# A recurrent layer with a low-rank adapter on one core: the adapter's weight by rows of 8 KB, its bias by 8 partitions, x one block earlier

## The chip, the core and the metric

The kernel runs on one core of a Trainium2 chip. The metric is the device time of one execution, in microseconds (us). The core has a matrix engine (PE, with its weight loads shown as PEld), a vector engine (DVE), a scalar engine (ACT), a further engine (POOL) and SP, which only issues DMA transfers here. Sixteen DMA engines move the data. Each engine carries out its own instructions in order and waits on semaphores that others raise; a transfer raises its semaphore by 16 when all of it has landed.

## What is computed

The reference, cut to what matters (B = 16, T = 256, D = H = 256, rank R = 8):

```python
xz = x @ Wx + b                                   # [16, 256, 1024]
for t in range(256):                              # the recurrence
    z = xz[:, t] + h @ Wh                         # h: [16, 256], Wh: [256, 1024]
    i, f, o, g = split(z)
    c = sigmoid(f) * c + sigmoid(i) * tanh(g)
    h = sigmoid(o) * tanh(c);  hs[:, t] = h
x = x + hs
n = layernorm(cond) * gamma + beta                # [16, 256]
w = gelu(n @ W1 + bias1) @ W2 + bias2             # W2: [256, 8192], 8 MB
a1, b1, a2, b2 = split(w)                         # each [16, 256, 8], one per batch entry
u = einsum("btd,bdr->btr", x, a2)
mid = gelu(x @ base_down + einsum("btr,blr->btl", u, b2))
v = einsum("blr,btl->btr", b1, mid)
out = x + mid @ base_up.T + einsum("bkr,btr->btk", a1, v)
```

All data are float32.

## The kernel before

**The recurrence** sets the pace. Time is cut into 32 blocks of 8 steps (`one_block(k, front)` of each engine, `s` from 0 to 7; step number 8k + s). In a step PE multiplies the hidden state with `wh` (line 712) on top of a projection that ACT has copied into PSUM (`seed_bank`, `seed_o`, lines 358 and 362), DVE transposes the result (lines 868 and 872), ACT applies the tanh, DVE forms the new cell and the new hidden state (lines 878 to 893), and PE begins again. Whatever else is to be done is placed by hand behind a step's own instructions on each engine: the transposes of later x (line 483), the projection of the block after next in 8 pieces (`project`, line 502; `PIECES` says which pieces fall into which step), its evacuation on DVE (line 802), the adapter for finished blocks (lines 515 to 590), and in the first four blocks `make_weights`.

**Ahead of step 0** `wx`, `wh` and other weights are loaded, x of blocks 0 and 1 is transposed and projected (block 1: pieces 0 to 5; its last two pieces come in step 0), and the projections go through DMA from `proj` into `seed`, whose layout the recurrence needs (`load_seed`, line 255, four transfers a block).

**The adapter's weight.** In block 0 the condition is normalised (DVE and POOL, line 1011), transposed and multiplied with `w1` (line 607, step 3); ACT's gelu gives `hid` (line 387). W2 comes in quarters, in the order `QUARTERS`, into three tiles; each quarter consists of four units (column half h, row half kc). From step 11 on PE multiplies one unit a step (line 633): steps 11 to 14 take quarter 0 of that order, 15 to 18 quarter 1, 19 to 22 quarter 2, 23 to 26 quarter 3. After every second unit DVE adds the bias (line 920; first at the end of step 12, after it has waited for all of `w_bias`), and POOL issues the transfers that put the result in its place (line 1020).

**SP's queue** is one list in order, and a waiting transfer holds up all behind it. Ahead of the blocks: x, `wx`, `wh`, x, gamma, beta, seed of block 0, x of block 2, W1, its bias, up, seed of block 1, down. In block 0: W2 pieces 0 and 1, x of block 3, pieces 2 to 7 with a transfer of the bias (line 289) behind each of 2 to 5, seed of block 2. In block 1: x of block 4, pieces 8 to 12, seed of block 3. In block 2: x of block 5, pieces 13 to 15, seed of block 4. A piece (`load_w2`, line 282) is two transfers of 256 KB, each 64 partitions by 4 runs of 1 KB; a transfer is only issued when the third before it has landed (`UNDER_WAY = 3`). Before PE's units wait just the two transfers of their own piece.

Of the kernel before, what the change touches and what calls it, by code (L numbers as in the profile page):

```python
# [26 lines left out]
P = 128  # L27
# [10 lines left out]
XQ = NQ  # L38
# [11 lines left out]


N_PIECES = 8
PIECES = ((0, 0, 0, 2, 2, 4, 5, 7, 8), (0, 1, 2, 3, 4, 5, 6, 7, 8), (0, 1, 2, 3, 4, 5, 6, 7, 8))
EVACUATE_AT = (1, 3, 5, 7)
N_X = 4
WARM_UP = 6
# [2 lines left out]
def lstm_adapter(nc, x, cond, Wx, Wh, b, base_up, base_down, gamma, beta, W1, bias1, W2, bias2, out):  # L59
    ctx = ExitStack()  # L60
    with ctx:
# [6 lines left out]
        def sem(name):  # L68
# [26 lines left out]
        c_norm = sb("c_norm", [B, D])  # L95
        c_stat = sb("c_stat", [B, 5])
        c_t = sb("c_t", [P, 2, B])
        w1 = sb("w1", [P, 2, D])
        b1_col = sb("b1_col", [P, 2])
        hid = sb("hid", [P, 2, B])  # L100
        w2_tiles = [sb(f"w2_{n}", [P, 2, D * RANK]) for n in range(3)]
# [44 lines left out]
        zeroed = sem("zeroed")  # L146
        w_loaded = {n: sem(f"{n}_loaded") for n in
                    ("wx_g", "wx_if", "wx_o", "wh_g", "wh_if", "wh_o", "b", "down", "up", "ln", "cond", "w1")}
        w2_loaded = [[[sem(f"w2_loaded{q}_{i}_{r}") for r in range(2)] for i in range(NQ)] for q in range(4)]
        w_bias_zeroed, w_bias_loaded = sem("w_bias_zeroed"), sem("w_bias_loaded")  # L150
        w_placed = [sem(f"w_placed{q}") for q in range(4)]
        wx_ready, wh_ready = sem("wx_ready"), sem("wh_ready")
# [86 lines left out]
        def _(sp):  # L239
# [27 lines left out]
                sp.dma_start(dst[:, :, lo:lo + n], src.rearrange(by_half, m=NM)[:, :, src_lo:src_lo + n])\  # L267
                  .then_inc(w_loaded[name], 16)

            w2_parts = W2.rearrange("(k p) (q j h n) -> q h k p j n", p=P, q=4, j=NQ, n=W_HALF)  # L270

            def load_w2(piece):

                n, i = divmod(piece, NQ)
                q, (h, kc) = QUARTERS[n], divmod(i, 2)
                if piece == 3 * NQ:
                    sp.wait_ge(w_psum, 2)
                for r, rows in enumerate((slice(0, P // 2), slice(P // 2, P))):
                    back, half = divmod(2 * piece + r - UNDER_WAY, 2)
                    if back >= 0:  # L280
                        sp.wait_ge(w2_loaded[QUARTERS[back // NQ]][back % NQ][half], 16)
                    sp.dma_start(w2[q][rows, kc, :].rearrange("p (j h n) -> p h j n", j=NQ, n=W_HALF)[:, h],
                                 w2_parts[q, h, kc, rows]).then_inc(w2_loaded[q][i][r], 16)

            bias_q = bias2.rearrange("(q j n) -> j q n", q=4, j=NQ)

            def load_w_bias(j):
                sp.wait_ge(w_bias_zeroed, 1)
                sp.dma_start(w_bias[32 * j:32 * j + B, :, :], bias_q[j].partition_broadcast(B)).then_inc(w_bias_loaded, 16)

            load_x(Blk(0, 0))
            load_cols(wx, Wx, 2 * H, 3 * H, H, "wx_g")
# [5 lines left out]
            load_x(Blk(0, 1))  # L298
            sp.dma_start(c_gamma[:, :], gamma.partition_broadcast(B)).then_inc(w_loaded["ln"], 16)
            sp.dma_start(c_beta[:, :], beta.partition_broadcast(B)).then_inc(w_loaded["ln"], 16)  # L300
            load_seed(Blk(0, 0))
            load_x(Blk(0, 0, 2))
            sp.dma_start(w1[:, :, :], W1.rearrange("(k p) n -> p k n", p=P)).then_inc(w_loaded["w1"], 16)
            sp.dma_start(b1_col[:, :], bias1.rearrange("(k p) -> p k", p=P),
                         allow_slow_non_contiguous=True).then_inc(w_loaded["w1"], 16)
            load_cols(up_raw, base_up, 0, 0, D, "up")
            load_seed(Blk(0, 1))
            load_cols(down, base_down, 0, 0, D, "down")
# [1 line left out]
            def one_block(k, front):  # L310
                if not k.at_least(1):
                    load_w2(0)
                    load_w2(1)
                if k.plus(3).exists():
                    load_x(k.plus(3))
                for piece in {0: range(2, 8), 1: range(8, 13), 2: range(13, 4 * NQ)}.get(k.k, ()):
                    load_w2(piece)
                    if 2 <= piece < 2 + NQ:
                        load_w_bias(piece - 2)
                if front:  # L320
                    load_seed(k.plus(2))
                done = follower(k.plus(-1))
                if done and done.seq.exists():
                    store_y(done)
                if early(k):
                    store_y(early(k))
# [12 lines left out]
        def _(act):  # L339
# [39 lines left out]

            def make_weights(k, s):  # L380

                if k == 0 and s == 3:

                    act.wait_ge(w_loaded["w1"], 32)
                    act.wait_ge(hidden_psum, 1)
                    for i in range(2):
                        act.activation(hid[:, i, :], aux[:, i * B:(i + 1) * B], ACT.Gelu,
                                       bias=b1_col[:, i:i + 1]).then_inc(hidden_ready, 1)
                if k == 0 and s in (4, 5):
                    act.wait_ge(up_psum, s - 3)  # L390
                    act.activation(up_t[:, s - 4, :], out_bank[:, 0:D], ACT.Copy).then_inc(up_ready, 1)
                if k == 2 and s in (2, 6):
                    n = s // 4
                    act.wait_ge(wt_psum, n + 1)
                    act.activation((a2_w, b1_w)[n][:, :, :], aux[:, 0:2 * P].rearrange("p (l t) -> p l t", l=2),
                                   ACT.Copy).then_inc(wt_ready, 1)
# [16 lines left out]
            def one_block(k, front):  # L413
                a, e, done = follower(k), early(k), follower(k.plus(-1))
                for s in range(TB):
# [31 lines left out]
                        act.wait_ge(ht_ready[1], n + 1)  # L447
                        seed_o(ahead.par, s_next)

                    if s == 1 and not k.at_least(1):  # L450
                        evacuate_x(k.plus(2))
                    if not k.at_least(EARLY + 2):
                        make_weights(k.k, s)
# [24 lines left out]
        def _(pe):  # L478
# [115 lines left out]
            def make_weights(k, s):  # L594
# [5 lines left out]
                        ins = pe.transpose(aux[:, i * B:(i + 1) * B], c_norm[:, i * P:(i + 1) * P], ident[0:B, 0:B])  # L600
                    ins.then_inc(cond_t_psum, 1)
                if k == 0 and s == 3:
                    pe.wait_ge(w_loaded["w1"], 32)
                    pe.wait_ge(cond_t_ready, 1)
                    for i in range(2):
                        for kc in range(2):
                            ins = pe.matmul(aux[:, i * B:(i + 1) * B], w1[:, kc, i * P:(i + 1) * P], c_t[:, kc, :],
                                            start=(kc == 0), stop=(kc == 1))
                    ins.then_inc(hidden_psum, 1)
                if k == 0 and s in (4, 5):  # L610
# [8 lines left out]
                if 0 <= k * TB + s - W_FIRST < 4 * NQ:  # L619


                    n, i = divmod(k * TB + s - W_FIRST, NQ)
                    q, (h, kc) = QUARTERS[n], divmod(i, 2)
                    if n == 0 and i == 0:
                        pe.wait_ge(hidden_ready, 2)
                        pe.wait_ge(up_ready, 2)
                    elif kc == 0:
                        pe.wait_ge(w_biased, 2 * n + h)
                    for half in w2_loaded[q][i]:
                        pe.wait_ge(half, 16)  # L630
                    for j in range(NQ):
                        first = W_COLS * j + W_HALF * h
                        ins = pe.matmul(out_bank[32 * j:32 * j + B, 0:W_HALF], hid[:, kc, :],  # L633
                                        w2[q][:, kc, first:first + W_HALF], start=(kc == 0), stop=(kc == 1))
                    if kc == 1:
                        ins.then_inc(w_psum, 1)
# [35 lines left out]
                ins.then_inc(b_psum, 1)  # L672
            project(Blk(0, 0), range(N_PIECES))
            transpose_x(Blk(0, 1), both)
            project(Blk(0, 1), range(6))

            pe.wait_ge(w_loaded["wh_if"], 16)
            pe.wait_ge(w_loaded["wh_o"], 16)
# [2 lines left out]
            def one_block(k, front):  # L681
# [3 lines left out]
                for s in range(TB):  # L685
# [65 lines left out]
                    if front:  # L751
                        if not k.at_least(1):
                            if s == 0:
                                project(Blk(0, 1), range(6, N_PIECES))
                            if s == 1:
                                transpose_x(f, both)
                        project(f, range(pieces[s], pieces[s + 1]))
                    if not k.at_least(EARLY + 2):
# [38 lines left out]
        def _(dve):  # L797
# [60 lines left out]
            dve.wait_ge(ln_step, 5)  # L858
            dve.tensor_scalar(c_stat[:, 3:4], c_stat[:, 2:3], 1.0 / D, LN_EPS, ALU.mult, ALU.add).then_inc(ln_step, 1)

            for q in range(XQ - 1):
                evacuate_projection(Blk(0, 1), q)
            dve.wait_ge(consts_made, 2)
            dve.reduce_sum(own_row[:, :], ident[:, :].rearrange("p (b r) -> p b r", b=B), AX.X).then_inc(zeroed, 1)
# [31 lines left out]
            def make_weights(k, s):  # L896
# [14 lines left out]
                if 0 <= u < 2 * NQ and not between:  # L911
                    n, h = divmod(u, 2)
                    dve.wait_ge(w_psum, u + 1)
                    if u == 0:
                        dve.wait_ge(w_bias_loaded, 16 * NQ)
                    if h == 0 and n >= 2:
                        dve.wait_ge(w_placed[QUARTERS[n - 2]], W_PLACED)
                    pairs = "p (d r) -> p d r"
                    dst = w_nat[n % 2][:, :, W_HALF // RANK * h:W_HALF // RANK * (h + 1)]
                    dve.tensor_tensor(dst.rearrange("p r d -> p d r"),  # L920
                                      out_bank[:, 0:W_HALF].rearrange(pairs, r=RANK),
                                      w_bias[:, QUARTERS[n], W_HALF * h:W_HALF * (h + 1)].rearrange(pairs, r=RANK),
                                      ALU.add).then_inc(w_biased, 1)
# [5 lines left out]
            def one_block(k, front):  # L929
                a, e, f, done = follower(k), early(k), k.plus(2), follower(k.plus(-1))  # L930
                for s in range(TB):
# [22 lines left out]
                        mask_v(a, mid_bank[a.lane])  # L954
                    if s == 2 and deferred(k) and done and done.seq.exists():
                        add_residual(done)
                    if s == 0 and not k.at_least(1):
                        evacuate_projection(Blk(0, 1), XQ - 1)
                    if front and k.at_least(1) and s in EVACUATE_AT:
                        if s == EVACUATE_AT[-1]:  # L960
                            h_free(k.plus(1))
# [22 lines left out]
        def _(pool):  # L984
# [22 lines left out]
                pool.memset(seed[i][:, :, :], 0.0).then_inc(seeds_zeroed, 1)  # L1007
            pool.memset(w_bias[:, :, :], 0.0).then_inc(w_bias_zeroed, 1)
            pool.wait_ge(w_bias_zeroed, 1)
            pool.wait_ge(ln_step, 6)  # L1010
            pool.tensor_tensor(c_stat[:, 4:5], c_stat[:, 3:4], neg_half[:, :], ALU.pow).then_inc(ln_pow, 1)

# [40 lines left out]
```

## Time and profile before

| | us |
|---|---|
| median of 3 runs | 602.84 |
| lowest and highest of them | 602.08, 607.48 |
| the profiled execution | 606.49 |
| its span, first to last instruction | 604.70 |
| PE busy in it | 584.7 (97%) |
| DVE busy | 502.5 (83%) |
| ACT busy | 384.6 (64%) |

The busy time of PE is an average over stages, and matmuls are pipelined, so it says little of where time can be had. The profile comes from one execution, and its times in the sections below count from the first instruction. "issue" as the cause of a wait means that the engine waited for nothing that the profile shows.

### The profile page before, as it was taken

How to read it: one execution, taken by the hardware profiler on the slowest of the kernel's cores; microseconds unless marked ns; L12 is line 12 of the kernel's file. 1: busy time of each engine (PE TensorE's matmuls, PEld its weight loads, DVE VectorE, ACT ScalarE, POOL GpSimd, SP SyncE). 2: the span in 40 equal slices, each digit the busy share in tenths (PEclk: the TensorE clock that was granted, in tenths of full speed). 3: DMA queues.
4: the chain of work that ended last, by engine and by line, in shares of the span. 5: the costliest groups of instructions: out<-in, count | busy, mean ns of one | idle time of the engine just before them, and what ended most of it. 6: DMA issues, size and time to landing. Idle time of an engine off the chain costs nothing.

```text
span 604.7 us, 34273 instructions
## 1 busy us (share of the span) xinstructions
PE 584.7 (97%) x14116; PEld 440.1 (73%) x14116; DVE 502.5 (83%) x2810; ACT 384.6 (64%) x2155; POOL 47.4 (8%) x91
## 2 busy tenths in 40 slices
PE   8888989999999999999999999999999999999997
PEld 7555557777777777777777777777777777777886
DVE  4667768888888888888888888888888888888874
ACT  2555546666666666666666666666666666666663
POOL 4002122000000000000000000000000000000000
PEclk9989899999999999999999999999999999999999
DMA  7999872123332212323221132332123333212201
GB/s 195 184 179 179 174 148 45 33 37 56 56 56 56 41 27 48 55 56 56 56 42 37 37 55 57 55 56 40 40 35 56 55 56 55 45 37 26 56 21 29
DMA packets 40158, 39.75 MB, mean 66 GB/s; under 512 B 4369, under 2 KB 38977, under 8 KB 40002
## 3 DMA queue, kind: packets, MB, share of 16 engines
q1 hardware_dynamic: 39456, 37.01, 33.7%
q8 instruction: 112, 1.84, 1.4%
q0 software_dynamic: 512, 0.53, 0.5%
q14 instruction: 44, 0.36, 0.3%
q10 hardware_dynamic: 34, 0.02, 0.0%
HBM read 16.05 MB, written 4.19 MB: 33 GB/s over the span
## 4 chain that ended last, share of the span: by engine, by line
PE 93%; DVE 2%; issue 2%; DMA 2%; SPq 0%; ACT 0%; DVEq 0%; ACTq 0%
PE z L712 35%; PE x_bank L502 18%; PE z_o L712 9%; PE aux L531 8%; PE out_bank L558 7%; PE aux L515 3%; PE aux L483 2%; PE out_bank L590 2%; PE aux L538 2%; PE out_bank L633 1%; DMA x_nat<-in_x 1%; DMA seed<-proj 1%; PE out_bank L579 1%; PE x_bank L579 1%; PE x_bank L531 0%
## 5 line engine op out<-in xcount | busy, mean ns | idle before, releaser
L712 PE MATMUL z<-wh,h_t 128*16 128x96 f32 x8160 | 235.5, 249 | 5.4 <-issue 3.4
L712 PEld LDWEIGHTS z<-wh,h_t 128*16 128x16 f32 x8160 | 154.2, 96 | 110.6 <-DVE h_t L893 79.8
L868 DVE STREAM_TRANSPOSE z<-z 128x96 f32<-128x96 f32 x512 | 152.4, 298 | 71.1 <-PE z L712 47.8
L422 ACT ACTIVATE gates<-z 128x48 f32<-128x48 f32 x512 | 108.1, 211 | 122.5 <-DVE z L868 122.3
L502 PE MATMUL x_bank<-wx,x_t 128*128 128x256 f32 x512 | 153.6, 387 | 0.6 <-ACT x_t L352 0.5
L358 ACT ACTIVATE z<-seed 128x96 f32<-128x96 f32 x512 | 126.9, 248 | 4.2 <-DMA seed<-proj 4.2
L712 PE MATMUL z_o<-wh,h_t 128*16 128x64 f32 x4080 | 105.6, 220 | 4.9 <-issue 4.9
L878 DVE SCALAR_TENSOR_TENSOR prod<-gates 128x32 f32<-128x32 f32 x512 | 98.2, 192 | 0.3
L712 PEld LDWEIGHTS z_o<-wh,h_t 128*16 128x16 f32 x4080 | 80.7, 97 | 5.4 <-issue 5.3
L502 PEld LDWEIGHTS x_bank<-wx,x_t 128*128 128x128 f32 x512 | 79.1, 192 | 4.2 <-ACT x_t L352 0.7
L428 ACT ACTIVATE gate_o<-z_o 128x32 f32<-128x32 f32 x256 | 50.6, 198 | 31.7 <-DVE z_o L872 6.4
L362 ACT ACTIVATE z_o<-seed 128x64 f32<-128x64 f32 x256 | 58.3, 228 | 19.3
L872 DVE STREAM_TRANSPOSE z_o<-z_o 128x64 f32<-128x64 f32 x256 | 65.7, 257 | 5.1 <-PE z_o L712 5.0
L1001 POOL TENSOR_TENSOR xp<-x_t,h_t 128x128 f32<-128x128 f32 (+1 forms) x60 | 30.3, 527 | 473.7 <-DVE h_t L893 456.6
L434 ACT ACTIVATE z_o<-z 128x16 f32<-128x16 f32 x256 | 43.0, 168 | 25.6
L802 DVE TENSOR_TENSOR proj<-x_bank,b_all 128x256 f32<-128x256 f32 x128 | 54.0, 422 | 2.4 <-PE x_bank L502 2.3
L883 DVE SCALAR_TENSOR_TENSOR z<-prod 128x16 f32<-128x16 f32 x256 | 46.7, 182 | 8.7
L888 DVE SCALAR_TENSOR_TENSOR gates<-prod 128x32 f32<-128x32 f32 x255 | 46.9, 184 | 0.0
L434 ACT ACTIVATE tanc<-tanc 128x16 f32<-128x16 f32 x256 | 45.6, 178 | 0.0
L893 DVE SCALAR_TENSOR_TENSOR h_t<-gate_o,z_o 128x16 f32<-128x16 f32 x256 | 43.7, 171 | 0.1
L893 DVE SCALAR_TENSOR_TENSOR h_t<-gate_o,tanc 128x16 f32<-128x16 f32 x256 | 43.7, 171 | 0.0
L531 PE MATMUL aux<-xp,down 128*128 128x128 f32 x232 | 43.3, 289 | 0.0
(137 smaller groups left out, 521.9 us busy)
## 6 DMA issues: line engine op xcount, KB each, us to landing
seed<-proj SPq DMA_DIRECT2D x128, 128.0 KB, 4.4
w<-in_L_cond_W SPq DMA_DIRECT2D x33, 256.0 KB, 4.8
x_nat<-in_x SPq DMA_DIRECT2D x32, 128.0 KB, 4.1
out<-y_nat SPq DMA_DIRECT2D x32, 128.0 KB, 4.1
wx<-in_L_cond_Wx SPq DMA_DIRECT2D x2, 256.0 KB, 3.9
wx<-in_L_cond_Wx SPq DMA_DIRECT2D x1, 512.0 KB, 4.8
wh<-in_L_cond_Wh SPq DMA_DIRECT2D x2, 256.0 KB, 5.7
wh<-in_L_cond_Wh SPq DMA_DIRECT2D x1, 512.0 KB, 6.0
```

The costliest lines, as they stand in the source:

```text
L358: act.activation(z_bank[m][:, 0:GC], seed[buf][:, s, P * m:P * m + GC], ACT.Copy)\
L362: act.activation(o_bank[:, 0:OC].rearrange("p (m c) -> p m c", c=C), seed[buf][:, s, :].rearrange("p (m q) -> p m q", m=NM)[:, :, GC:P], A ...
L422: act.activation(gates[s % 2][m][:, 0:3 * B].rearrange("p (g b) -> p g b", b=B), zt[m].rearrange("p (g c) -> p g c", c=C)[:, :, 0:B], ACT. ...
L434: act.activation(tanc[m], cell[m], ACT.Tanh, scale=0.5).then_inc(tanc_ready[m], 1)
L502: ins = pe.matmul(x_bank[q % 2][:, 0:XW].rearrange("p (m g c) -> p m g c", m=NM, c=C), x_t[f.k % N_X][:, kc, :], wx[:, kc, :].rearrange("p ...
L531: ins = pe.matmul(mid_bank[a.lane][:, cols], lhs, rhs, start=(part == 0), stop=(part == 2))
L712: ins = pe.matmul(dst, h_prev[:, kc, :], rhs, start=False, stop=(kc == 1), skip_group_check=True)
L802: dve.tensor_tensor(proj[f.par][:, q * XW:(q + 1) * XW], x_bank[q % 2][:, 0:XW], b_all[:, q * XW:(q + 1) * XW], ALU.add).then_inc(xz_ready, 1)
L868: dve.transpose(zt[m], z_bank[m][:, 0:GC]).then_inc(turned[m], 1)
L872: dve.transpose(zt_o, o_bank[:, 0:OC]).then_inc(turned_o, 1)
L878: dve.scalar_tensor_tensor(prod[m][:, :], now[:, 0:2 * B], 1.0, now[:, 2 * B:4 * B], ALU.add, ALU.mult).then_inc(prod_ready[m], 1)
L893: dve.scalar_tensor_tensor(h_t[k.par][:, m, s, 0:B], gate_o[:, B * m:B * (m + 1)], 1.0, tanc[m], ALU.add, ALU.mult).then_inc(ht_ready[m], 1)
```

## The change

W2 is loaded by rows: a piece i of a quarter is again two transfers of 256 KB (kc = 0 and 1), now each 32 partitions of one run of 8 KB. Its source pattern takes the rows of W2 as (k, i, r, e) with e = 8 in front of r = 4, so that the hidden units stand in another order on the partitions. To match it ACT copies `w1` with its columns in that order into `w1_turned` in step 2, which line 607 then reads, and `bias1` is loaded in that order by POOL in eight transfers. PE's first unit of a quarter now waits for all eight transfers of it. The bias of W2 comes in eight transfers of 8 partitions instead of four of 16, one behind each of pieces 2 to 9, and DVE's first addition waits for all eight. x of block 2 is loaded ahead of the first seed, x of block 4 behind piece 4, and from block 1 on x of block k + 4 is loaded where x of block k + 3 was. Block 1 is projected whole ahead of step 0; x of block 2 is transposed in step 0 instead of 1, and the pieces of block 0 are spread otherwise.

```diff
-PIECES = ((0, 0, 0, 2, 2, 4, 5, 7, 8), (0, 1, 2, 3, 4, 5, 6, 7, 8), (0, 1, 2, 3, 4, 5, 6, 7, 8))
+PIECES = ((0, 0, 2, 3, 3, 4, 5, 7, 8), (0, 1, 2, 3, 4, 5, 6, 7, 8), (0, 1, 2, 3, 4, 5, 6, 7, 8))
...
-            w2_parts = W2.rearrange("(k p) (q j h n) -> q h k p j n", p=P, q=4, j=NQ, n=W_HALF)
+            w2_rows = W2.rearrange("(k i r e) (q n) -> q k i e r n", k=2, i=NQ, e=8, q=4)
             def load_w2(piece):
                 n, i = divmod(piece, NQ)
-                q, (h, kc) = QUARTERS[n], divmod(i, 2)
+                q = QUARTERS[n]
...
-                for r, rows in enumerate((slice(0, P // 2), slice(P // 2, P))):
-                    back, half = divmod(2 * piece + r - UNDER_WAY, 2)
+                for kc in range(2):
+                    back, kc_back = divmod(2 * piece + kc - UNDER_WAY, 2)
                     if back >= 0:
-                        sp.wait_ge(w2_loaded[QUARTERS[back // NQ]][back % NQ][half], 16)
-                    sp.dma_start(w2[q][rows, kc, :].rearrange("p (j h n) -> p h j n", j=NQ, n=W_HALF)[:, h],
-                                 w2_parts[q, h, kc, rows]).then_inc(w2_loaded[q][i][r], 16)
+                        sp.wait_ge(w2_loaded[QUARTERS[back // NQ]][back % NQ][kc_back], 16)
+                    sp.dma_start(w2[q][32 * i:32 * (i + 1), kc, :], w2_rows[q, kc, i]).then_inc(w2_loaded[q][i][kc], 16)
...
-            def load_w_bias(j):
+            def load_w_bias(n):
+                first = 32 * (n // 2) + B // 2 * (n % 2)
                 sp.wait_ge(w_bias_zeroed, 1)
-                sp.dma_start(w_bias[32 * j:32 * j + B, :, :], bias_q[j].partition_broadcast(B)).then_inc(w_bias_loaded, 16)
+                sp.dma_start(w_bias[first:first + B // 2, :, :], bias_q[n // 2].partition_broadcast(B // 2))\
+                  .then_inc(w_bias_loaded, 16)
...
+            load_x(Blk(0, 0, 2))
             load_seed(Blk(0, 0))
-            load_x(Blk(0, 0, 2))
...
-            sp.dma_start(b1_col[:, :], bias1.rearrange("(k p) -> p k", p=P),
-                         allow_slow_non_contiguous=True).then_inc(w_loaded["w1"], 16)
...
-                if k.plus(3).exists():
+                if not k.at_least(1):
                     load_x(k.plus(3))
+                elif k.plus(4).exists():
+                    load_x(k.plus(4))
                 for piece in {0: range(2, 8), 1: range(8, 13), 2: range(13, 4 * NQ)}.get(k.k, ()):
                     load_w2(piece)
-                    if 2 <= piece < 2 + NQ:
+                    if piece == 4:
+                        load_x(k.plus(4))
+                    if 2 <= piece < 2 + 2 * NQ:
                         load_w_bias(piece - 2)
...
+                if k == 0 and s == 2:
+                    act.wait_ge(w_loaded["w1"], 16)
+                    act.activation(w1_turned[:, :, :].rearrange("p k (i e r) -> p (k i) e r", i=8, e=8),
+                                   w1[:, :, :].rearrange("p k (i r e) -> p (k i) e r", i=8, e=8), ACT.Copy)\
+                       .then_inc(w1_ready, 1)
...
-                    if s == 1 and not k.at_least(1):
+                    if s == 0 and not k.at_least(1):
                         evacuate_x(k.plus(2))
...
-                    for half in w2_loaded[q][i]:
-                        pe.wait_ge(half, 16)
+                    if i == 0:
+                        for part in w2_loaded[q]:
+                            for half in part:
+                                pe.wait_ge(half, 16)
...
-            project(Blk(0, 1), range(6))
+            project(Blk(0, 1), range(N_PIECES))
...
-                                project(Blk(0, 1), range(6, N_PIECES))
-                            if s == 1:
                                 transpose_x(f, both)
...
-            for q in range(XQ - 1):
+            for q in range(XQ):
                 evacuate_projection(Blk(0, 1), q)
...
-                        dve.wait_ge(w_bias_loaded, 16 * NQ)
+                        dve.wait_ge(w_bias_loaded, 2 * 16 * NQ)
...
-                    if s == 0 and not k.at_least(1):
-                        evacuate_projection(Blk(0, 1), XQ - 1)
...
+            b1_rows = bias1.rearrange("(k i r e) -> k i e r", k=2, i=NQ, e=8)
+            for kc in range(2):
+                for i in range(NQ):
+                    pool.dma_start(b1_col[32 * i:32 * (i + 1), kc:kc + 1], b1_rows[kc, i],
+                                   allow_slow_non_contiguous=True).then_inc(b1_loaded, 16)
```

## Rows read from the trace of the kernel before

**Rows 1.** The page's slices: DMA load, tenths, 40 slices of 15.1 us.

```profile
DMA  7999872123332212323221132332123333212201
```

**Rows 2.** Two stretches: length, busy us of each engine, granted clock, DMA share, GB/s.

```profile
30.00:45.00 15.00, 12.01 (x290) 8.47 (x290) 9.99 (x55) 7.48 (x42) 1.01 (x2) 0.89 0.99 180
105.00:120.00 15.00, 15.00 (x379) 11.28 (x370) 13.10 (x75) 10.32 (x58) 0.02 (x1) 1.00 0.12 30
```

**Rows 3.** Timeline of PE, starts of steps 0, 8, 9, 17, 18, 19, 28.

```profile
17.23 0.85 PE L712 MATMUL z<-wh,h_first 128*16 128x96 f32 x32 [1.29 <-ACT z L358]
...
38.76 1.48 PE L712 MATMUL z<-wh,h_t 128*16 128x96 f32 x32
...
41.74 0.98 PE L712 MATMUL z<-wh,h_t 128*16 128x96 f32 x32
...
62.91 1.53 PE L712 MATMUL z<-wh,h_t 128*16 128x96 f32 x32
...
66.39 0.84 PE L712 MATMUL z<-wh,h_t 128*16 128x96 f32 x32
...
68.94 0.86 PE L712 MATMUL z<-wh,h_t 128*16 128x96 f32 x32
...
93.47 0.95 PE L712 MATMUL z<-wh,h_t 128*16 128x96 f32 x32
```

**Rows 4.** Timeline of PE later, starts of two steps, four apart.

```profile
300.48 0.95 PE L712 MATMUL z<-wh,h_t 128*16 128x96 f32 x32
...
309.33 0.91 PE L712 MATMUL z<-wh,h_t 128*16 128x96 f32 x32
```

**Rows 5.** Waits of PE, 17 to 95 us: us in all, times, longest.

```profile
PE z_o L712 <- issue: 4.9, 2, 2.5
PE z L712 <- issue: 3.4, 2, 2.5
...
PE aux L483 <- DMA x_nat<-in_x: 0.4, 1, 0.4
```

**Rows 6.** Waits of all engines, 95 to 590 us: PE's own row for issue.

```profile
PEld aux L515 <- issue: 6.7, 28, 0.2
```

**Rows 7.** DMA queues of the page: packets, MB, share.

```profile
q8 instruction: 112, 1.84, 1.4%
```

**Rows 8.** Timeline of SP's queue: start, us, line, transfers issued.

```profile
6.67 0.41 SPq L300 DMA_DIRECT2D c_beta<-in_L_cond_ln_beta  x1
10.07 3.02 SPq L255 DMA_DIRECT2D seed<-proj  x4
...
21.14 5.72 SPq L282 DMA_DIRECT2D w<-in_L_cond_W  x4
...
48.11 2.55 SPq L255 DMA_DIRECT2D seed<-proj  x4
...
51.35 16.03 SPq L282 DMA_DIRECT2D w<-in_L_cond_W  x10
```

**Rows 9.** Landing of line 282's transfers (W2), then of line 289's (bias).

```profile
DMA to landing us min/median/max: 3.8/5.0/6.9
...
DMA to landing us min/median/max: 4.7/5.6/6.0
```

**Rows 10.** Two stretches as in rows 2, early loads and W2.

```profile
5.00:8.00 3.00, 3.00 (x15) 2.86 (x15) 0.63 (x1) 0.30 (x1) 1.75 (x2) 1.00 1.03 344
51.50:66.50 15.00, 12.12 (x272) 7.68 (x264) 10.42 (x55) 7.10 (x41) 3.25 (x6) 0.89 0.92 177
```

**Rows 11.** Timeline of DVE: first addition of the bias.

```profile
50.81 0.63 DVE L920 TENSOR_TENSOR w_nat<-out_bank,w_bias 128x256 f32<-128x256 f32 x1
```

**Rows 12.** Line 399 on ACT: ns min/median/max, first and last start.

```profile
L399 ACT ACTIVATE wh<-wh x1: 631/631/631, 8.3 to 8.3; 128x512 f32<-128x512 f32 x1
```

**Rows 13.** POOL: an issue's ns (line 1020), then POOL's next instruction.

```profile
L1020 POOL DMA_DIRECT2D b_t<-w_nat x4: 524/544/562, 78.8 to 80.3; - x4
...
14.58 0.56 POOL L1011 TENSOR_TENSOR c_stat<-c_stat,neg_half 16x1 f32<-16x1 f32 x1 [7.82 <-DVE c_stat L859]
```

More of the change, by code:

```diff
@@ L97, in lstm_adapter @@
         c_t = sb("c_t", [P, 2, B])
-        w1 = sb("w1", [P, 2, D])
+        w1, w1_turned = sb("w1", [P, 2, D]), sb("w1_turned", [P, 2, D])
         b1_col = sb("b1_col", [P, 2])
@@ L148, in lstm_adapter @@
                     ("wx_g", "wx_if", "wx_o", "wh_g", "wh_if", "wh_o", "b", "down", "up", "ln", "cond", "w1")}
-        w2_loaded = [[[sem(f"w2_loaded{q}_{i}_{r}") for r in range(2)] for i in range(NQ)] for q in range(4)]
+        w1_ready, b1_loaded = sem("w1_ready"), sem("b1_loaded")
+        w2_loaded = [[[sem(f"w2_loaded{q}_{i}_{kc}") for kc in range(2)] for i in range(NQ)] for q in range(4)]
         w_bias_zeroed, w_bias_loaded = sem("w_bias_zeroed"), sem("w_bias_loaded")
@@ L380, in make_weights @@
             def make_weights(k, s):
+                if k == 0 and s == 2:
[3 more added lines that the diff above has]
+                       .then_inc(w1_ready, 1)
                 if k == 0 and s == 3:
-                    act.wait_ge(w_loaded["w1"], 32)
+                    act.wait_ge(b1_loaded, 16 * 2 * NQ)
                     act.wait_ge(hidden_psum, 1)
@@ L602, in make_weights @@
                 if k == 0 and s == 3:
-                    pe.wait_ge(w_loaded["w1"], 32)
+                    pe.wait_ge(w1_ready, 1)
                     pe.wait_ge(cond_t_ready, 1)
@@ L606, in make_weights @@
                         for kc in range(2):
-                            ins = pe.matmul(aux[:, i * B:(i + 1) * B], w1[:, kc, i * P:(i + 1) * P], c_t[:, kc, :],
+                            ins = pe.matmul(aux[:, i * B:(i + 1) * B], w1_turned[:, kc, i * P:(i + 1) * P], c_t[:, kc, :],
                                             start=(kc == 0), stop=(kc == 1))
```

## The prediction

> **What bounds the kernel now.** I read the page's slices first, then the stretches, the waits, and the timelines of the engines and of SP's queue. The slices show a DMA load of 0.7 to 0.9 and more up to about 90 us, then 0.1 to 0.3 [rows 1]. The stretches say what that does to PE: between 30 and 45 us it is busy 12.0 of 15 us at a DMA share of 0.99, with a mean granted clock of 0.89; between 105 and 120, at a share of 0.12, 15.0 of 15 us at 1.00 [rows 2]. So the early phase is slower than the rest. By how much is read from the starts of the steps: step 0 begins at 17.23, step 28 at 93.47, that is 76.2 us for 28 steps [rows 3], against (309.33 - 300.48) / 4 = 2.2 us a step later on [rows 4]. 28 x 2.2 = 61.6, so 14.6 us are lost between steps 0 and 28; the change touches this phase and what lies ahead of it.
>
> Where the 14.6 us lie: PE waits 4.9 + 3.4 = 8.3 us for "issue" in four gaps, the longest 2.5 us, and 0.4 us for x_nat [rows 5]; from 95 to 590 us no PE row but the 0.2 us ones of its weight loads names issue [rows 6]. Two of the gaps are followed by matmuls that take 1.48 and 1.53 us where 0.85 to 0.95 is usual, in stretches with a lowered granted clock [rows 2, 3]: steps 8 and 17 take 41.74 - 38.76 = 2.98 and 66.39 - 62.91 = 3.48 us, together 2.1 us too long [rows 3]. Step 18, with the transposes of w_tmp in it, takes 68.94 - 66.39 = 2.55 us [rows 3]; such real extra work, 0.35 us, stands in four steps (18, 24, 25, 26), 1.35 in all. The remaining 2.5 us are spread thinly, most of it over steps 2, 3 and 15.
>
> A gap with nothing waited for, and only under a saturated DMA, looks like late instructions: queue 8 brings 112 packets and 1.84 MB of them [rows 7]. The Trainium skill ("Runtime: NRT & Kernel Launch", section "Instruction fetch mechanics") says that an engine's instructions come through a DMA queue in 16 KiB blocks, mostly hidden. The trace agrees in size (1.84 MB / 112 = 16.4 KB) and not in "hidden", if the gaps are such fetches; if they are not, nothing is gained at them, which is rival C below.
>
> **The change part by part.**
>
> *W2 in 32 transfers of 32 rows of 8 KB, three under way as before.* The bytes and the count of transfers stay; rows of 1 KB become rows of 8 KB, and the source pattern's leading size becomes 8. The pace T per transfer is the number that matters. Before: ten issues took 16.0 us, T = 1.6 [rows 8]. No row shows a data row of 8 KB or a leading size of 8, so bounds: from below, three under way and a landing of at least 3.8 us give 3.8 / 3 = 1.27 [rows 9]; from above, if only eight of the 16 engines shared a transfer at the rate of the loaded stretch (177 GB/s / 0.92 / 16 = 12 GB/s each), 256 KB / 8 / 12 = 2.7 us [rows 10]. I take 1.4, near the lower end: the early loads, in rows of 1 and 2 KB, reach 344 GB/s [rows 10], so the engines themselves don't hold W2 at 177, and even eight engines at 344 / 16 = 21.5 GB/s give 1.5. If the gaps come from instruction packets queued behind W2's 1 KB rows, they should go: 1,024 rows in place of 8,192. That is worth between 0 and 8.3 + 2.1 us, and I take all of it, less surely than any other step.
>
> *Bias in eight transfers, one behind each of pieces 2 to 9.* DVE's first addition of the bias (line 920, end of step 12) now waits for all eight. Six are issued in block 0, but the last two follow pieces 8 and 9 in block 1, hence stand behind load_seed of block 2, load_x of block 5 and four more W2 transfers on SP's in-order queue. Behind the waiting instruction on DVE stand the transposes of step 13, so the whole recurrence stops. Before, all four stood ahead of the seed of block 2 on SP [rows 8], and the addition at 50.81 waited for nothing [rows 11]. After, in order of time: the seed of block 1 is complete earlier (its last projection moves ahead of step 0), so down goes out at about 18.2 and W2 starts at 18.85 instead of 21.14 [rows 8]; the fourth transfer waits for the first to land, which I put at 4.7 (between 3.8 and 5.0 [rows 9]), 23.55; twelve more at T, and five biases of a quarter of a transfer: 23.55 + 12 x 1.4 + 5 x 0.35 = 42.1; the sixth bias 0.65, four seed issues 2.55 [rows 8], x 0.65: transfer 17 at 45.95; transfer 20 when 17 has landed, 3 x 1.4 later, 50.15; the last bias 0.65 later, 50.8, landed 4.2 later (one of twice the size took 4.7 to 6.0 [rows 9]): **t = 55.0**. In general t = 28.05 + 19.25 T. DVE would be ready at about 17.2 + 13 x 2.2 + 0.2 = 46, so it waits some 9 us, which swallows whatever the first 12 steps gain.
>
> *PE waits for a whole quarter at its first unit.* Quarters 0 to 2 are early: transfer 24 lands at 50.15 + 4 x 1.4 + 4.2 = 60, against step 19 at 55 + 6 x 2.2 = 68. Quarter 3: load_seed of block 3 waits for the evacuation at the end of step 15, 55.0 + 6.6 = 61.6; then 3.2 us of issues, transfer 27 at 64.8, 32 at 64.8 + 4.2 + 2 x 1.4 = 71.8, landed 76.0; step 23 comes at 55 + 22.35 = 77.4. So 0, with 1.4 us to spare; at T = 1.6 it is even.
>
> *Projection of block 1 whole ahead of step 0:* four matmuls, some 1.1 us, into PE's idle 1.29 us before step 0 [rows 3]: 0 to 0.1 of delay. Step 0 loses them and one DVE addition; with the evened pieces the first steps gain about 0.5, swallowed by the bias wait. *x earlier:* an issue of 0.6 us where SP has nothing to issue from 7.08 to 10.07 [rows 8]; the 0.4 us wait goes. *w1_turned on ACT:* 512 columns as in line 399, 0.63 us [rows 12]; ACT is busy 7.5 of 15 us here [rows 2], and the x evacuation has moved from step 1 to step 0: 0, at worst (strided, double) 0.6, swallowed too. *b1 by eight POOL issues:* 8 x 0.54 = 4.4 us from 6.76 on, done at 11.1; POOL's next instruction waits for DVE until 14.58 [rows 13]. So 0; without that cover the normalisation in step 0 would come 4.4 us late.
>
> **The sum.** From DVE's resuming at t to step 28 it takes 33.0 (15 steps of 2.2) + 1.35 of real extra work - 0.25 (how far PE's step 13 starts ahead of DVE's addition) = 34.1, plus 1.0 for a lowered clock after the long wait (steps 8 and 17 lost 0.8 and 1.3). From step 28 to the end nothing changes: 604.70 - 93.47 = 511.2; 606.49 - 604.70 = 1.8 lie outside the span. 55.0 + 34.1 + 1.0 + 511.2 + 1.8 = 603.1, against 606.49 of the same execution, 3.4 less. The median shown is 602.84, 3.65 below the profiled run, about one gap and its slow step; the runs spread from 602.08 to 607.48. If that offset is constant, 599.4 follows; if it is a gap that the new wait covers anyway, 603.1. I take 600.5, between.
>
> **The rivals.**
> *B, the bias comes early enough and the gain shows.* A gain of over 6 us asks for t under 52, T under 1.25. With no bias wait at all: 606.49 - (14.6 - 1.35) = 593.2, or 589.6 by the median. For it: early loads at 344 GB/s. Against it: the landing floor of 3.8 us, and the order on SP's queue.
> *C, the gaps stay.* Rows get longer but the engines stay full. Gaps up to step 12 hide under the bias wait; the two later ones cost 2 x 2.5 us, with slow steps 7 in all: 603.1 + 7 = 610, or 606.5 by the median. For it: load and gaps go together [rows 2, 5, 6]. Against it: far fewer packets.
> *D, slower: eight engines carry W2 at their loaded pace.* T = 2.7, t = 80; then quarter 3 decides: transfer 26 at 71 + 6 x 2.7 = 87, transfer 27 at 90, the last landing at 112, step 23 there, step 28 at 124 instead of 93.5: 31 us more, 637, or 634 by the median. It decides from T = 1.9 (t = 64.6, 6 us more than now); below T = 1.55 nothing is lost. Against it: the same engines move 21.5 GB/s each between 5 and 8 us [rows 10].
> The Trainium skill ("DMA: Bandwidth & Descriptors", section "Why a DMA increments its semaphore by 16 and not by 1") says that such a transfer uses the largest number of engines, at most 16, that divides the leading sizes of both its patterns, and the lowest-numbered ones. By that, W2 and its bias would use eight engines and leave eight free: D if the eight are slow, no gaps at all if the instruction packets travel on the other eight, C if not. No row here shows which engine a packet took.
>
> **How the numbers follow.** The forecast (gaps gone, the bias wait in their place, within 1%) 0.48; B 0.24; C 0.16, half of it beyond +1%; D and other slow paces 0.12, 0.10 of it beyond. About 1%, 6 us, is what a measurement of this kernel can tell from no change. Faster by over 1%: 0.24; slower by over 1%: 0.08 + 0.10 = 0.18; the rest, 0.58, within. The range takes in T from 1.27 (t = 52.5, 597 to 600.6), the nearer half of B (593), C's 610 and the beginning of D: 593 to 611; the forecast's own range is 597 to 605.
>
> **What would show it.** Right: a wait of DVE's line 920 for w_bias of 5 to 12 us between 46 and 58 us, no issue gaps of 2 us on PE, W2 issues about 1.4 us apart, no wait for W2 at steps 11, 15, 19 and 23, an unchanged pace after 100 us. Wrong: line 920 waits for nothing (B); issue gaps after step 13 (C); PE waiting at line 633, W2 issues 2 us and more apart (D).

## The result and the profile after

The changed kernel takes 622.63 us (median of 4 runs, 620.79 to 624.10) against 603.12 us: a ratio of 1.0308, 95% interval 1.025 to 1.0365. It is slower by 3%, and lies above the 611 us at which the range given ends. Its profiled execution took 620.79 us with a span of 619.0.

The page's slices of the changed kernel, to be read against [rows 1]:

```profile
PEclk9996689999999999999999999999999999999999
DMA  7857564332123232321233333212233323112311
```

The DMA load is no longer 0.9 but 0.5 to 0.8 in the early phase, and the phase ends later. The clock line has two slices of 0.6. The stretches of [rows 2] again (busy us of PE, PEld, DVE, ACT, POOL, then granted clock, DMA share, GB/s), and a later one:

```profile
30.00:45.00 15.00, 13.47 (x360) 9.00 (x356) 12.60 (x73) 10.15 (x58) 1.01 (x2) 1.00 0.51 181
45.00:60.00 15.00, 4.13 (x116) 2.46 (x108) 2.32 (x14) 1.89 (x11) 0.00 (x0) 0.70 0.70 145
60.00:75.00 15.00, 8.65 (x176) 5.34 (x176) 7.25 (x37) 4.81 (x28) 2.57 (x5) 0.62 0.44 136
...
105.00:120.00 15.00, 14.84 (x386) 11.25 (x378) 12.64 (x72) 9.51 (x54) 3.09 (x6) 1.00 0.33 50
```

Between 30 and 45 us PE is now busy for 13.5 us where it was 12.0. That alone doesn't make it the work of the change: in a second execution of the kernel before, shown below, it is 13.46 us. The DMA share there is 0.51 at 181 GB/s, where the kernel before had 0.99 at 180. Half the share at the same rate fits a W2 that occupies half of the engines, each of which moves twice as much; a count of packets below bears out the number of engines. Then PE is busy 4.1 of 15 us. The waits of the changed kernel, first of all engines, then of PE (us in all, times, longest):

```profile
DVE w_nat L929 <- DMA w_bias<-in_L_cond_bias: 17.9, 1, 17.9
...
PE out_bank L644 <- DVE w_nat L929: 17.0, 1, 17.0
...
PE aux L656 <- DMA w_tmp<-w_nat: 2.2, 1, 2.2
PE x_bank L511 <- issue: 0.8, 1, 0.8
...
PE out_bank L644 <- issue: 0.2, 1, 0.2
```

The forecast wait is there, DVE's line 929 (920 before) for w_bias, and it is 17.9 us long. PE stands 17.0 us of that behind it. Of the issue gaps of [rows 5] 0.8 and 0.2 us are left. Where the bias stays so long is read from SP's queue (start, us, line, transfers issued):

```profile
19.43 6.60 SPq L283 DMA_DIRECT2D w<-in_L_cond_W  x4
...
46.86 0.48 SPq L290 DMA_DIRECT2D w_bias<-in_L_cond_bias  x1
47.52 2.66 SPq L256 DMA_DIRECT2D seed<-proj  x4
50.22 0.60 SPq L245 DMA_DIRECT2D x_nat<-in_x  x1
50.87 4.27 SPq L283 DMA_DIRECT2D w<-in_L_cond_W  x2
55.18 0.46 SPq L290 DMA_DIRECT2D w_bias<-in_L_cond_bias  x1
56.45 4.29 SPq L283 DMA_DIRECT2D w<-in_L_cond_W  x2
60.78 0.47 SPq L290 DMA_DIRECT2D w_bias<-in_L_cond_bias  x1
```

The last bias is issued at 60.78, behind a seed, an x and four transfers of W2, of which two pairs take 4.3 us each. The chain that ended last (first four rows) and the timeline of PE show what it costs (start, us):

```profile
50.87 9.17 DMA w<-in_L_cond_W
...
60.78 4.57 DMA w_bias<-in_L_cond_bias
65.44 0.59 DVE w_nat L929
...
74.05 9.69 DMA w_tmp<-w_nat
...
18.35 0.85 PE L723 MATMUL z<-wh,h_first 128*16 128x96 f32 x32 [0.65 <-ACT z L362]
...
47.32 0.96 PE L723 MATMUL z<-wh,h_t 128*16 128x96 f32 x32
...
67.40 1.48 PE L723 MATMUL z<-wh,h_t 128*16 128x96 f32 x32 [0.26 <-DVE h_t L902]
...
71.22 0.96 PE L723 MATMUL z<-wh,h_t 128*16 128x96 f32 x32
...
78.36 0.96 PE L723 MATMUL z<-wh,h_t 128*16 128x96 f32 x32
...
84.16 0.85 PE L723 MATMUL z<-wh,h_t 128*16 128x96 f32 x32
...
107.45 0.94 PE L723 MATMUL z<-wh,h_t 128*16 128x96 f32 x32
```

Step 0 begins at 18.35 and step 13 at 47.32, 2.23 us a step: hardly anything is lost there, where [rows 3] has a step of 2.98 us (8 to 9). Then step 14 begins at 67.40, and its matmuls take 1.48 us. PE had stood still for 17 us, and the granted clock was at 0.62 in the stretch from 60 to 75, part of it at the lower of the two levels (1.2 of 2.4 GHz). Step 18, with the transposes of w_tmp, lasts from 78.36 to 84.16. Step 28 begins at 107.45 instead of 93.47, and from there to the end it is 511.5 us as before (511.2).

### The profile page after: what moved, and what is told of

Read it like the earlier page. It is cut to its first block, busy times and chain, and to the rows that moved or that the text cites. A ratio compares the mean times of both kernels' runs of the same rounds, so it can differ in the third digit from the quotient of the medians.

```text
span 619.0 us, 34284 instructions
## 1 busy us (share of the span) xinstructions
PE 586.3 (95%) x14116; PEld 440.4 (71%) x14116; DVE 503.1 (81%) x2810; ACT 385.3 (62%) x2156; POOL 51.8 (8%) x99
## 4 chain that ended last, share of the span: by engine, by line
PE 87%; DMA 8%; DVE 2%; SPq 1%; issue 1%; POOL 1%; ACT 0%; DVEq 0%
PE z L723 32%; PE x_bank L511 17%; PE z_o L723 8%; PE aux L540 8%; PE out_bank L567 7%; DMA w<-in_L_cond_W 6%; PE aux L524 3%; PE out_bank L599 2%; PE aux L492 2%; PE aux L547 2%; DMA w_tmp<-w_nat 2%; PE out_bank L644 1%; DMA w_bias<-in_L_cond_bias 1%; PE out_bank L588 1%; PE x_bank L588 1%
## 5 line engine op out<-in xcount | busy, mean ns | idle before, releaser
L723 PE MATMUL z_o<-wh,h_t 128*16 128x64 f32 x4080 | 104.1, 219 | 0.0
```

What stands on the lines that cost most here:

```text
L723: ins = pe.matmul(dst, h_prev[:, kc, :], rhs, start=False, stop=(kc == 1), skip_group_check=True)
```

## The experiments

Each kernel is measured against the kernel before on the same chip.

**The bias early, in the changed kernel.**

```diff
-                    if 2 <= piece < 2 + 2 * NQ:
-                        load_w_bias(piece - 2)
+                    if 2 <= piece < 2 + NQ:
+                        load_w_bias(2 * (piece - 2))
+                        load_w_bias(2 * (piece - 2) + 1)
```

Expected: 

> The changed kernel, but the eight bias transfers go out two behind each of pieces 2 to 5, all in block 0. Theory 1 (two waits in a row: first the bias, and behind it PE's wait for a whole quarter of W2): DVE's wait of 17.9 us for w_bias goes, but W2's transfers keep their pace of 1.6 us and are held up some 5 us by each block's seed and x, so PE then waits at the first unit of quarters 2 and 3 for W2, 5 to 10 us each; 606 to 613 us. Rival (the bias wait is the whole loss): no wait for W2 over 2 us, 590 to 598 us.

Measured: 623.0 us, ratio 1.0305 (1.0246 to 1.0364). DVE's wait is gone, and not a microsecond is won. The longest waits of PE and of ACT for data in that kernel:

```profile
PE out_bank L645 <- DMA w<-in_L_cond_W: 20.7, 3, 15.9
ACT z L363 <- DMA seed<-proj: 13.0, 3, 6.6
```

PE waits 20.7 us for W2 at the first units of quarters, the longest 15.9, and ACT waits for seeds three times. Theory 1 holds in kind (a second wait stood right behind the first) and is too mild in size.

**Outer dimension 16 instead of 8, bias early.**

```diff
-            w2_rows = W2.rearrange("(k i r e) (q n) -> q k i e r n", k=2, i=NQ, e=8, q=4)
+            w2_rows = W2.rearrange("(k i r e) (q n) -> q k i e r n", k=2, i=NQ, e=16, q=4)
```

(the columns of `w1_turned` and `bias1` follow in the same order). Expected: 

> As the kernel with the bias early, but the source rows of W2 (and of bias1 and w1's turned columns) with an outer dimension of 16 instead of 8; rows of 8 KB as there. Theory (the issue gaps of PE went because half the DMA engines stay free of W2): each W2 transfer raises its semaphore from 16 engines, the DMA share is near 1 again in the W2 phase, and PE has at least two issue gaps of over 1.5 us; 2 to 8 us slower than with the outer dimension of 8. Rival (the gaps went because of fewer, longer rows): no issue gap over 1 us, and the same time within 2 us.

Measured: 614.53 us, ratio 1.0168 (1.0104 to 1.0232): 8.5 us faster than with 8, the opposite of what I expected. Queue 1 of the page, which carries W2, for outer dimension 8 (bias early) and then for 16 (packets, MB, share):

```profile
q1 hardware_dynamic: 31760, 37.01, 31.2%
```

```profile
q1 hardware_dynamic: 32016, 37.01, 33.5%
```

The same bytes take 256 packets more, eight for each of W2's 32 transfers, as one closing packet for each of eight more engines would give. So the outer dimension did set the number of engines. No issue gap is over 1 us with 16 either, so half of the engines need not be free for that; but this is one execution each, and the kernel before has one without gaps too (below). The stretch from 47.5 to 60 us, in which a seed, an x and W2 share the queue, for outer dimension 8 and then for 16:

```profile
40.00:47.00 7.00, 5.82 (x159) 3.45 (x157) 5.31 (x32) 3.79 (x23) 0.00 (x0) 1.00 0.54 184
47.50:60.00 12.50, 7.98 (x185) 4.22 (x184) 6.35 (x35) 3.76 (x22) 2.16 (x4) 0.90 0.77 124
```

```profile
40.00:47.00 7.00, 6.21 (x180) 3.86 (x170) 5.79 (x34) 4.34 (x26) 0.00 (x0) 1.00 0.79 179
47.50:60.00 12.50, 8.04 (x194) 4.40 (x192) 6.88 (x41) 4.61 (x29) 2.25 (x5) 0.95 0.92 153
```

While W2 is nearly alone (40 to 47) both deliver about 180 GB/s, one at a share of 0.54 and the other at 0.79. With the seed and x among it, 8 gives 124 GB/s and 16 gives 153; the kernel before gave 172 in that stretch. The same is seen at W2's last six transfers on SP's queue, behind the seed of block 3 and an x, for 8 and then for 16 (start, us):

```profile
75.70 15.22 SPq L283 DMA_DIRECT2D w<-in_L_cond_W  x6
```

```profile
74.23 9.96 SPq L283 DMA_DIRECT2D w<-in_L_cond_W  x6
```

PE's wait for W2 is 7.1 us instead of 20.7.

**The bias late, alone, in the kernel before.**

```diff
-                    if 2 <= piece < 2 + NQ:
+                    if 2 <= piece < 2 + 2 * NQ:
                         load_w_bias(piece - 2)
...
-                        dve.wait_ge(w_bias_loaded, 16 * NQ)
+                        dve.wait_ge(w_bias_loaded, 2 * 16 * NQ)
```

(with `load_w_bias` by 8 partitions, as in the change). Expected: 

> The kernel before, with one part of the change: the bias in eight transfers of 8 partitions, one behind each of pieces 2 to 9. Theory (the place on SP's queue makes the wait, whatever the form of W2): DVE waits for w_bias at the end of step 12 until about 62 us, some 11 us; the issue gaps that fall into that wait cost nothing more; 609 to 615 us. Rival (it needs the slower landing of the new W2 transfers): a wait under 4 us, 602 to 607 us.

Measured: 615.81 us, ratio 1.0192 (1.0129 to 1.0255), with

```profile
DVE w_nat L922 <- DMA w_bias<-in_L_cond_bias: 17.0, 1, 17.0
```

The place on the queue makes the wait with either form of W2; it is 17 us instead of the 11 that I gave it, and the time lies just above the 609 to 615 us expected.

**The whole quarter, alone, in the kernel before.**

```diff
-                    for half in w2_loaded[q][i]:
-                        pe.wait_ge(half, 16)
+                    if i == 0:
+                        for part in w2_loaded[q]:
+                            for half in part:
+                                pe.wait_ge(half, 16)
```

Expected: 

> The kernel before, with one part of the change: PE's first unit of a quarter waits for all eight transfers of it. Theory (the whole quarter is a cost of its own, since the last transfer of quarter 3 landed at 84.6 us and its first unit ran at 82.8): PE waits for W2 at step 23 for 3 to 8 us, of which a gap or a late x would have taken some anyway; 604 to 610 us. Rival (hidden behind the gaps): no wait over 1 us, 602 to 604 us.

Measured: 612.26 us, ratio 1.0142 (1.0105 to 1.0179), with

```profile
PE out_bank L635 <- DMA w<-in_L_cond_W: 5.6, 1, 5.6
PE aux L483 <- DMA x_nat<-in_x: 3.1, 1, 3.1
```

So this part alone costs 9 us, which the prediction had put at 0; the time lies above the 604 to 610 us expected here.

**x and the projection, alone, in the kernel before.** All lines of the change that concern `load_x`, `PIECES`, `project`, `evacuate_x` and `evacuate_projection`, nothing else. Expected: 

> The kernel before, with one part of the change: x loaded earlier, block 1 projected whole ahead of step 0, the pieces of block 0 spread otherwise; W2, its bias and bias1 as before. Theory: steps 0 to 3 lose some 0.5 us of delay and PE's 0.4 us wait for x goes, the issue gaps stay: 0.5 to 1.5 us faster than before, 601 to 603 us. Rival (starting W2 earlier also shifts the gaps): a change of 2 us or more either way.

Measured: 603.53 us, ratio 1.0004 (0.997 to 1.0037). No change. In the execution that was profiled, the slowest of the ten with 607.52 us, the gaps are gone all the same (none over 0.7 us); PE waits 3.8 us for W2 instead, and ACT 9.5 us in all for seeds. That pointed away from the gaps, to the delivery.

**The kernel before once more.** Expected: 

> The kernel before, unchanged, profiled once more. Theory 1 (the issue gaps belong to this order of work): the four gaps, 8 us in all, come again at the same steps 5, 7, 16 and 23, within a step. Theory 2 (they differ from execution to execution): the sum of PE's issue gaps differs by more than 3 us from 8.3, while the span stays within 3 us of 604.7, so that the gaps aren't what sets the time.

Measured: 603.8 us, span 602.0. PE's waits from 17 to 95 us:

```profile
PE aux L483 <- DMA x_nat<-in_x: 5.4, 1, 5.4
PE z L712 <- DVE h_t L893: 2.2, 5, 0.8
PE z L712 <- ACT z L358: 1.3, 1, 1.3
PE aux L515 <- POOL xp L1001: 0.6, 1, 0.6
```

Not one issue gap, where [rows 5] has 8.3 us of them; 5.4 us of waiting for x_nat stand in their place, and the span is 2.7 us shorter. Theory 2: the gaps come and go, and of their 8.3 us the time follows by 2.7. The stretch from 30 to 45 us, to be read against [rows 2]:

```profile
30.00:45.00 15.00, 13.46 (x355) 8.76 (x347) 12.99 (x75) 10.18 (x58) 1.00 (x2) 1.00 0.98 184
```

PE is as busy there as in the changed kernel, at a DMA share of 0.98.

**Six transfers under way, in the kernel before** (`UNDER_WAY = 6`). Expected: 

> The kernel before, with six transfers under way instead of three and nothing else. Theory (W2 to 64 partitions is bound by where it lands, not by the chain): distance still 1.4 to 1.6 us in the quiet stretches, the seeds land later; 601 to 606 us. Rival (the chain of three is the bound): distance about 1 us, 595 to 600 us.

Measured: 616.87 us, ratio 1.0195 (1.0129 to 1.0262), and PE's waits:

```profile
PE z L712 <- issue: 9.6, 4, 4.5
PE z_o L712 <- issue: 4.9, 1, 4.9
```

and the end of the longest gap in PE's timeline:

```profile
40.43 0.61 PE L712 MATMUL z_o<-wh,h_t 128*16 128x64 f32 x11 [4.86 <-issue]
```

14.5 us of gaps, and the kernel is 14 us slower; PE waits for no W2 and no x. Neither branch was right: the time is not set by the pace, it grows by what the gaps add up to. What PE waits for in a gap is told by the DMA packets in the traces. Before this gap ends, a packet of queue 8, the instructions of [rows 7], runs from 37.25 to 38.67 us. All 31 gaps of 0.4 us and more that PE shows between 17 and 100 us, in 11 of the 13 traces, end 1.3 to 1.8 us after a packet of that queue has ended. So the gaps are waits for instructions. That these come late because data are queued ahead of them stays an inference. For it: in this run the packets begin 9 us apart (37.2, 46.4, 55.9), in the kernel before 5 to 8. Against a simple rule: six transfers to all 128 partitions (below) give no gap over 2.4 us.

**All 128 partitions, in the kernel before.** A transfer has two of the four runs for all partitions, instead of four runs for half of them.

```diff
-                for r, rows in enumerate((slice(0, P // 2), slice(P // 2, P))):
+                for r in range(2):
...
-                    sp.dma_start(w2[q][rows, kc, :].rearrange("p (j h n) -> p h j n", j=NQ, n=W_HALF)[:, h],
-                                 w2_parts[q, h, kc, rows]).then_inc(w2_loaded[q][i][r], 16)
+                    sp.dma_start(w2[q][:, kc, :].rearrange("p (j h n) -> p h j n", j=NQ, n=W_HALF)[:, h, 2 * r:2 * r + 2],
+                                 w2_parts[q, h, kc][:, 2 * r:2 * r + 2]).then_inc(w2_loaded[q][i][r], 16)
```

Expected: 

> The kernel before, with each W2 transfer over all 128 partitions and two of the four runs of 1 KB, instead of 64 partitions and four runs; 256 KB, three under way, order and bias as before. Theory (the early phase is bound by the delivery of W2, and a transfer to a part of the partitions can't use the full rate that the early loads of 128 partitions show): issue distance of W2 1.1 to 1.3 us instead of 1.5 to 1.6, last landing before 78 us instead of 84.6; gaps or no gaps, 3 to 8 us faster: 595 to 600 us. Rival (the pace is set by HBM or by the seeds between): the distance stays at 1.5, 601 to 605 us.

Measured: 597.82 us, ratio 0.9881 (0.9805 to 0.9957): faster than both kernels. SP's ten issues of block 1, to be read against [rows 8], and the stretch from 47.5 to 60:

```profile
50.18 13.56 SPq L282 DMA_DIRECT2D w<-in_L_cond_W  x10
...
47.50:60.00 12.50, 11.41 (x316) 7.06 (x310) 10.69 (x57) 7.04 (x42) 3.28 (x6) 1.00 0.83 200
```

13.6 us for ten instead of 16.0 (1.36 each, between the two branches), and 200 GB/s at a share of 0.83 instead of 172 at 0.98. Part of the first difference is spread, since the second execution of the kernel before took 14.4 us; but from W2's first issue to its last it is 54 us here, and 59 and 60 in the two executions of the kernel before. PE's waits from 17 to 95 us are 1.4 us for x and twice 0.2 us for issue, beside the recurrence's own. Three additions to it: six under way. Expected: 

> As the run with all 128 partitions, with six transfers under way instead of three. Theory (delivery is bound by the chain where the transfers are fast): a distance of under 1 us in the quiet stretches and W2 complete by 72 us; 593 to 599 us, not slower than with three. Rival (seed and x then land later behind six transfers): ACT waits over 2 us for a seed or PE for x, 601 to 608 us.

Measured: 603.9 us, ratio 1.0006 (0.9973 to 1.0039), with 6.6 us of issue gaps again. The time is the rival's, its waits are not: ACT waits for no seed and PE for no x. Four under way. Expected: 

> The run with all 128 partitions, with four transfers under way instead of three. Theory (more under way lengthens PE's issue gaps and the landing of the seeds, as six did): 597 to 603 us, PE's issue gaps over 1 us again. Rival (four are the better balance): 592 to 597 us without gaps.

Measured: 598.59 us, ratio 0.9929 (0.99 to 0.9959), 3.5 us of gaps in all; in time no different from three. And x with the projection on top. Expected: 

> The run with all 128 partitions plus the part of the change that moves x and the projection. Theory (that part alone gave no gain because W2's delivery stood behind it; with a faster delivery its earlier x takes away the wait for x_nat, 1.4 us, and the seeds come no later): 594 to 598 us. Rival (it starts W2 earlier and no more): within 1 us of the run with 128 partitions alone, or slower.

Measured: 598.04 us, ratio 0.9902 (0.987 to 0.9933), no different from 128 partitions alone.

## Why the prediction was wrong

From the 600.5 us of the forecast to 622.63 it is 22 us. Of these, 10.4 lie in t, 6.9 between t and step 28, and 0.3 behind that. The other 4.4 are the offset from the profiled execution to the median: the forecast took 2.6 us off, and it turned out as 1.8 on top.

**Right in its place and cause, wrong in size: the bias wait.** That the last two biases stand behind the seed and four transfers, and that DVE then stops the recurrence at the end of step 12, came as said, for 17.9 us instead of some 9. The sum mis-sized its term t: 55.0 was forecast, 65.4 measured. Transfer 17 went out at 50.87 instead of 45.95. The start (19.43 for 18.85) and a first wait longer than 4.7 us are part of that; so are two transfers of x among the 16, which the working left out. From transfer 17 to the last bias it took 9.9 us instead of 4.85. There the step that failed is "transfer 20 when 17 has landed, 3 x 1.4 later": transfer 17 took 9.2 us to land instead of 4.2. The working took one pace for all stretches, and in this one a seed and an x move beside W2, so that two pairs took 4.3 us each. Eight engines are not the whole of it: with the old form of W2 the bias late came to a wait of 17.0 us too.

**Wrong: the 34.1 us from t to step 28.** It took 107.45 - 65.44 = 42.0 us, 35.1 with the clock's 1.0. Step 14 alone lasted 71.22 - 67.40 = 3.8 us, after 17 us of standstill. Step 18 lasted 84.16 - 78.36 = 5.8 us where 2.55 had been put: the transfers that place the adapter's results landed late (9.7 us in the chain, where those of line 1020 took at most 5.8 before), and PE waited 2.2 us for w_tmp. The sum had no term for transfers other than W2 that land late.

**Wrong: "worth between 0 and 8.3 + 2.1 us, and I take all of it".** This step moved neither t nor the way from there to step 28; it is the reading of the early phase, and with it rival B, that fails. The reading of a gap as late instructions holds (the packets of queue 8, above). The changed kernel's profile shows 1.0 us of gaps, and steps 0 to 13 at 2.23 us each. But the gaps weren't a loss that could be had: 8.3 us of them came and went between two executions of the same kernel that differ by 2.7 us, and with the x and projection part alone they went without gain. That longer rows took them away isn't shown either, since the kernel before has one execution without them. What the runs point to as the limit of the early phase is the delivery of W2, seeds and x: a wait for x or a seed stands where a gap is missing, and a faster delivery of W2 alone is worth 5 us (128 partitions). The exception is a longer queue, where the gaps grow beyond that (six under way).

**Right in the number by luck: "So 0, with 1.4 us to spare" for the wait for a whole quarter.** Alone it costs 9 us. In the changed kernel no such wait shows, since the bias wait gives W2 17.9 us to catch up; take that away and 20.7 us of it appear. So a part's price can't be read by taking it out of the whole: bias late alone 1.9%, whole quarter alone 1.4%, the whole change 3.1%, the change without the late bias still 3.1%, because one wait hides the other. Of the 20 us that are left without the late bias, 8.5 go with 16 engines instead of eight; the rest, 11 us, is little more than the 9 us of the whole quarter alone.

**Rival D came nearest, for another reason.** W2 did use eight engines, by the 256 packets that 16 add. The Trainium skill ("DMA: Bandwidth & Descriptors", section "Why a DMA increments its semaphore by 16 and not by 1") states this number for a leading size of 8; the share of 0.51 at 181 GB/s agrees. They weren't slow: nearly alone they carried what 16 carried. They lost where other transfers came between. The bound for T from the loaded stretch was no measure for them, and the range's end at 611 rested on it being unlikely. The same page of the Trainium skill (section "Rules for kernel authors") advises one transfer over 128 partitions instead of two over disjoint halves, which it says "serialize". The runs bear the advice out: halves take 602.7 us and all partitions 597.8, for the same bytes and count of transfers. Rivals B and C did not come: the wait was longer than forecast, and the profile shows no gap over 0.8 us.

That eight engines cost 8.5 us beside sixteen is shown; why the rate falls from 153 to 124 GB/s with seed and x among it isn't. It may be that a transfer spread over all 16 engines lands only when the eight with the longer queue have done their share; that is not shown, as no view names the engine of a packet. The part of bias1 on POOL cost nothing, as said (its issues ran from 7.1 to 11.6 us, before POOL was needed). ACT's copy of w1 took 1.10 us, where line 399 takes 0.63 [rows 12]; the upper bound had been twice that.

## What to carry to other kernels

Where a phase is bound by delivery, the idle times of the engine aren't a sum that can be won: profile the kernel before twice, and see which of them come again, before pricing their removal or crediting a change with it. Two parts that both make a later step wait can hide each other: test each alone and the whole without it. A transfer that one engine will wait for needs its place in the queue worked out with everything ahead of it, and at the rate of the stretch in which that lies. Split a large load by columns over all 128 partitions rather than by partitions, and keep what is queued short where other transfers and instructions must pass.

## What was not expected of the hardware

Eight engines moved W2 in rows of 8 KB as fast as sixteen did in such rows (179 GB/s between 40 and 47 us) and had done in rows of 1 KB: 170 to 184 GB/s at a share of 0.48 to 0.54 while W2 was nearly alone. Transfers of 256 KB to 128 partitions raised the rate of the mixed stretch to 200 GB/s, against 172 for transfers of the same size to 64 partitions. A packet of instructions that comes late stops PE, and in these traces PE went on 1.3 to 1.8 us after the packet had ended. Six transfers under way instead of three cost 14 us where each went to 64 partitions (616.9 against 602.7 us) and 6 us where each went to 128 (603.9 against 597.8 us).
